# The prologue of a time-mix and mixture-of-experts kernel: low weight parts by subtraction, and the residual added by TensorE

## The reference

```python
for i in range(2):                                   # time mix, layer i
    normed = layer_norm(out, ln_w[i], ln_b[i])
    k, v = normed @ Wk[i].T, normed @ Wv[i].T
    r = sigmoid(normed @ Wr[i].T)
    state_t = 0.95 * state_{t-1} + 0.05 * (k * v)_t   # a scan over the tokens
    out = out + (r * state) @ Wo[i].T
x = layernorm(h + out)
# experts: each token goes to its 2 best experts of 8, each expert takes the first 307 rows
logits = x @ router_w + router_b
h_e = einp @ w_c_fc[e] + b_c_fc[e];  g_e = einp @ w_gate[e] + b_gate[e]
o_e = silu(h_e * g_e) @ w_c_proj[e] + b_c_proj[e]
x = layernorm(x + sum over the token's 2 experts of prob * o_e[its row])
```

## Time and profile before

| | |
|---|---|
| time before, median of 3 runs | 372.24 us (372.0 to 374.78) |
| the profiled execution's own time | 371.38 us |
| its span, first to last instruction | 369.4 us |
| PE busy | 331.3 us, 90% |
| DVE busy | 262.7 us, 71% |
| POOL busy | 194.9 us, 53% |
| ACT busy | 169.9 us, 46% |
| mean granted clock of TensorE | 0.983 of full speed |

### The profile page before, as it was taken

The page is one execution under the profiler, slowest core; times in us unless marked ns, Lnnn a source line. Parts: engine busy times, 40 slices in busy tenths (PEclk is TensorE's granted clock), DMA queues, the critical chain, the costliest instruction groups (busy, mean ns, idle before and its releaser), DMA issues.

```text
span 369.4 us, 7109 instructions
## 1 busy us (share of the span) xinstructions
PE 331.3 (90%) x2295; PEld 281.0 (76%) x2295; DVE 262.7 (71%) x851; ACT 169.9 (46%) x311; POOL 194.9 (53%) x240
## 2 busy tenths in 40 slices
PE   6979768678799999999999999999998999998980
PEld 2435354336697988999879879999998989988880
DVE  5487865757986677797868876989454688675535
ACT  1634425445454455455543635455554455555200
POOL 4021216871405565233346567784777755777762
PEclk9999979999999999999999999999999999999997
DMA  7902892435001311431111237222326712121152
GB/s 200 228 24 88 73 286 85 138 102 141 9 18 35 91 38 52 112 93 35 39 51 34 84 124 178 74 59 68 94 75 168 127 40 56 40 51 41 45 162 70
DMA packets 61245, 32.59 MB, mean 88 GB/s; under 512 B 15995, under 2 KB 58823, under 8 KB 61210
## 3 DMA queue, kind: packets, MB, share of 16 engines
q1 hardware_dynamic: 55866, 23.96, 26.9%
q0 software_dynamic: 4256, 7.94, 7.6%
q10 hardware_dynamic: 1088, 0.26, 0.4%
HBM read 19.01 MB, written 13.69 MB: 89 GB/s over the span
## 4 chain that ended last, share of the span: by engine, by line
PE 74%; DVE 9%; issue 5%; ACT 4%; POOL 3%; DMA 3%; POOLq 0%; DVEq 0%; ACTq 0%
PE ps_o L790 19%; PE bank L635 3%; PE pair1h L719 3%; PE bank L643 3%; PE bank L645 3%; PE pair1g L773 2%; PE pair0g L773 2%; PE ps_o L660 2%; DVE kv_sb L1096 2%; PE bank L751 2%; PE pair0g L774 2%; PE pair0g L775 2%; PE pair1g L775 2%; PE pair1g L774 2%; PE bank L615 2%
## 5 line engine op out<-in xcount | busy, mean ns | idle before, releaser
L790 PE MATMUL ps_o<-proj_sb,hidden 128*104 128x128 f32 x768 | 96.2, 273 | 0.2 <-DVE o_sb L1277 0.2
L1463 POOL DMA_INDIRECT slot_rows<-x_rows,row_to x64 | 71.4, 1116 | 42.5 <-DVE prod L1265 24.0
L790 PEld LDWEIGHTS ps_o<-proj_sb,hidden 128*104 128x104 f32 x768 | 90.2, 170 | 1.1 <-issue 0.7
L959 ACT ACTIVATE gate_s<-pair0g,bgate_sb 128x308 f32<-128x308 f32 x64 | 33.1, 517 | 73.6 <-PE pair0g L775 73.6
L1503 POOL DMA_INDIRECT picked<-expert_rows,row_from x48 | 49.8, 1037 | 31.0 <-DVE prod L1265 19.2
L1265 DVE SCALAR_TENSOR_TENSOR prod<-pair1h,bfc_sb,gate_s 128x308 f32<-128x308 f32 x64 | 34.0, 531 | 22.9 <-ACT gate_s L959 22.8
L966 ACT ACTIVATE hidden<-prod 128x616 f32<-128x616 f32 x64 | 45.5, 711 | 8.4 <-DVE prod L1265 8.4
L1265 DVE SCALAR_TENSOR_TENSOR prod<-pair0h,bfc_sb,gate_s 128x308 f32<-128x308 f32 x64 | 34.1, 532 | 14.7 <-ACT gate_s L959 14.2
L959 ACT ACTIVATE gate_s<-pair1g,bgate_sb 128x308 f32<-128x308 f32 x64 | 32.9, 515 | 24.0 <-PE pair1g L775 23.4
L1435 POOL TENSOR_SCALAR shifted<-moments 128x4 f32<-128x4 f32 x24 | 5.5, 231 | 69.0 <-DVE moments L1053 68.9
L773 PE MATMUL pair1g<-slotT_hi,gate_hi 128*128 128x308 f32 x64 | 26.0, 406 | 2.3 <-DVE prod L1265 2.2
(11 more groups left out here) (203 smaller groups left out, 766.3 us busy)
## 6 DMA issues: line engine op xcount, KB each, us to landing
slot_in<-slot_rows SPq DMA_DIRECT2D x20, 260.0 KB, 3.8
expert_rows<-o_sb SPq DMA_DIRECT2D x24, 156.0 KB
x_in<-in_L_attn_h SPq DMA_DIRECT2D x4, 512.0 KB, 5.2
x_rows<-in_L_ffn_w_gate SPq DMA_DIRECT2D x8, 256.0 KB, 4.2
...
```

Of the source, the lines that this page charges most:

```text
L790: mm = nc.tensor.matmul(ps_o[0:PART, P * part:P * part + P], hidden[:, e % 2, c, PART * part:PART * part + PART], proj_sb[:, e, c, :], sta ...
L959: nc.scalar.activation(gate_s[:, c % 2, :], pair[c % 2][0][:, 0:COLS], ACT.Identity, bias=bgate_sb[:, e, j:j + 1]).then_inc(g_copied, 1)
L1463: nc.gpsimd.indirect_dma_start(out=slot_rows, out_offset=bass.IndirectOffsetOnAxis(ap=row_to[:, c:c + 1], axis=0), in_=x_rows[:, b, c // K ...
```

## The change

It alters the prologue alone, and the tables of the periods stay. Its parts:

1. **Low parts by subtraction.** `split` on TensorE, `low` on ScalarE and the constant `minus` are gone. GpSimd subtracts for experts 0 and 1 and VectorE for experts 2 to 7, two subtractions of 128 by 512 for each expert (weight minus high part, all in SBUF). `high` is one entry for each matrix now. Loads of later experts wait for these subtractions.
2. **The residual added in PSUM.** A new stage `carry` on TensorE multiplies the residual by `ident` into the bank in which `out` then accumulates. Layer 1 needs 4 such products of 128 columns, layer 2 needs 8, since it adds `x_in` and `x_mid` (so `skip_sum` is gone for batches 0 and 1). `stats` reads the bank directly, and a new stage `added` on ScalarE copies it to SBUF in place of VectorE's `add`. Batch 0 alternates between two banks, `pair1h` and `ps_o`, and batch 1 uses the banks of its v products.
3. **Both halves turned first.** `turn` for both halves stands ahead of the two `kvr`, VectorE's `add` no longer stands between the halves, and the two turns and logits of the router have two banks.
4. **Order and fillers.** `FILL` has 18 fillers behind the first 12, in place of 23. `stats` of batch 2 moves from points 1 and 3 of the first period to the head of VectorE, and `stats` (1, 5) ahead of the slots. `load_x(2)` stands ahead of the loads of experts 4 to 7, and `load_expert(3)` behind the small biases.

The diff, cut to its core (of the lists a line each):

```diff
-TENSOR_HEAD = [("turn", 0, 0), ("kvr", 0, 0), ("turn", 0, 1), ("kvr", 0, 1), ("out", 0, 0), ("split", 0, 0),
+TENSOR_HEAD = [("carry", 0, 0), ("turn", 0, 0), ("carry", 0, 1), ("turn", 0, 1), ("kvr", 0, 0), ("kvr", 0, 1),
...
+               ("out", 0, 0), ("out", 0, 1), ("carry", 0, 2), ("turn", 0, 2), ("turn", 0, 3), ("kvr", 0, 2),
...
+               ("low", 7, 1), ("stats", 2, 0), ("stats", 2, 1), ("slots", 0, 0), ("slots", 0, 1),
...
+LOW_BY_POOL = 2
...
-FILL = {("weights", 0, 0): 12, ("turn", 0, 0): 5, ("kvr", 0, 0): 5, ("kvr", 0, 1): 1, ("turn", 0, 2): 3,
-        ("kvr", 0, 2): 4, ("kvr", 0, 3): 1, ("turn", 0, 4): 2, ("turn", 0, 5): 2}
+FILL = {("weights", 0, 0): 12, ("turn", 0, 0): 1, ("turn", 0, 3): 3, ("turn", 0, 4): 6, ("turn", 0, 5): 2, ("count", 0, 0): 6}
...
             if b >= 2:
                 return bank[1 + n % 2]
-            return ps_o
+            if b == 0:
+                return (pair[1][1], ps_o)[n % 2]
+            return mix_banks(b, n)[2]
...
-            return (ps_o,) * 3 if b == 0 else bank
+            return (pair[1][1], ps_o, pair[1][1]) if b == 0 else bank
...
             def load_expert(e):
-                if e >= 2:
-                    sp.wait_ge(weights_apart, 2 * (e - 1))
+                if 2 <= e < LOW_BY_POOL + 2:
+                    sp.wait_ge(pool_low_made, 2 * (e - 1))
+                elif e >= 2:
+                    sp.wait_ge(vector_low_made, 2 * (e - 1 - LOW_BY_POOL))
...
+            def carry(b, n):
+
+                if b == 1:
+                    pe.wait_ge(kv_made, step(b, n))
+                if n == 0:
+                    pe.wait_ge(x_loaded[b], 16)
+                if n > 1:
+                    pe.wait_ge(x_added, step(b, n - 2))
+                ps = out_bank(b, n)
+                for j in range(HT):
+                    t = HT * (n % 2) + j
+                    nc.tensor.matmul(ps[:, P * j:P * j + P], ident[:, :], x_in[:, b, t, :],
+                                     start=(j == 0), stop=False, skip_group_check=True)
+                    if n > 1:
+                        nc.tensor.matmul(ps[:, P * j:P * j + P], ident[:, :], x_mid[:, b, t, :],
+                                         start=False, stop=False, skip_group_check=True)
...
-                                          w_mix[:, 3 * L + n // 2, :], start=True, stop=True)
+                                          w_mix[:, 3 * L + n // 2, :], start=(b > 1), stop=True,
+                                          skip_group_check=(b < 2))
...
-            def split(e, which):
...
+            def added(b, n):
+
+                last = (n + 2) // 4
+                act.wait_ge(stats_made[last], step(b, n + 2))
+                act.wait_ge(out_made, step(b, n))
+                dst = x_mid if n < 2 else x_in
+                nc.scalar.activation(dst[:, b, HT * (n % 2):HT * (n % 2) + HT, :],
+                                     out_bank(b, n)[:, :].rearrange("p (j d) -> p j d", d=P), ACT.Copy)\
+                  .then_inc(x_added, 1)
...
-            def high(e, _):
+            def high(e, which):
...
-            def low(e, which):
...
-                    i = nc.vector.bn_stats(stats[:, r, norm, j, :], source_of(b, n)[:, j, :])
+                    i = nc.vector.bn_stats(stats[:, r, norm, j, :],
+                                           out_bank(b, n - 2)[:, P * (j % HT):P * (j % HT) + P] if summed
+                                           else source_of(b, n)[:, j, :])
...
+            def low_of(e, which):
+
+                dve.wait_ge(weights_high, 2 * e + which + 1)
+                nc.vector.tensor_tensor((gate_lo, fc_lo)[which][:, e, :].rearrange("p (j d) -> p j d", d=P),
+                                        w_in[:, e % 2, HC * which:HC * which + HC, :],
+                                        (gate_hi, fc_hi)[which][:, e, :].rearrange("p (j d) -> p j d", d=P).bitcast(F32),
+                                        ALU.subtract).then_inc(vector_low_made, 1)
...
-                    if b == 0 and point in (1, 3):
-                        stats_of(2, point // 2)
...
+            def low_of(e, which):
+
+                pool.wait_ge(weights_high, 2 * e + which + 1)
+                if e == 0:
+                    pool.wait_ge(state_made, step(0, 1))
+                else:
+                    pool.wait_ge(normed_made[0], step(0, 3))
...
```

152 lines of the change are left out of this document (74 added, 78 removed).

## The result

| | before | after |
|---|---|---|
| time, median | 372.46 us (372.0 to 374.78, 4 runs) | 363.89 us (363.4 to 364.26, 4 runs) |
| ratio | | 0.9771, 95% interval 0.9744 to 0.9797 |
| the profiled execution's own time | 371.38 us | 364.26 us |
| its span | 369.4 us | 362.4 us |
| first expert product starts | 90.48 us | 82.50 us |

The forecast was 363.5.

A forecast was written before the change was run, and what follows sets the result against it. TensorE, 90% busy, bounds the kernel, so gains lie in the prologue's waits. First product -8.7, holes -2.6, clock +2.3, VectorE's queue +0.3 sum to -8.7: profiled run 362.7, median 0.9 above, thus 363.5; range 360 to 368.

The forecast's parts named there:

- Batch 0's mixing: Prologue, batch 0's two layers: layer 1's norm ends 3.2 us earlier, layer 2's last norm 6.8 earlier, at 39.0.
- Routing: Prologue, router behind batch 0's mixing: logits end at 41.6, 8.5 us earlier; row numbers at 48.1, 8.4 earlier.
- Scatters: GpSimd's 16 scatters: 25.0 us as before plus 0.6 for VectorE's subtractions; slots loaded at 76.0, landed 79.2.
- GpSimd is dear: Rival: GpSimd's subtraction costs 2.4 or VectorE's subtractions stretch scatters by 4.4: 366 to 367.5, both 369 to 370; chance 0.18.
- Batch 1: Prologue: its last `out` ends at 72.4, or up to 5 us later by the clock (77.4), hidden by the slots at 79.2.
- The first product: Start of the expert stage: the first expert product starts at 81.8 against 90.48, -8.7 us.
- The holes: First period: TensorE's waits of 1.41 and 1.17 us behind VectorE close, -2.6.
- The clock in the last gap: TensorE idle from 73 to 79: clock falls to 1.2 GHz until about 86, slowing the first products, +2.3 us.
- After that the shift stays to the end: Periods behind the first points: TensorE is full as before, so the -8.7 us stays to the end.
- the periods take it back: Rival: the expert stage waits for something that doesn't move, up to 6 of the 8.7 us lost: 369.5; chance 0.05.
- The slower rival: Batch 1 in the prologue: the clock stays at 1.2 GHz throughout, 14 us left unhidden: about 375; chance 0.05.

The follow-up runs named there:

- the run at 371.4: The changed kernel with the two `rstd` of batch 1's second layer back behind the 10th and the 12th scatter: 371.41 us, ratio 0.9987.
- the run at 390: The kernel before with only the low parts by subtraction (no `split`, no `low` on ScalarE), all else as before: 390.08 us, ratio 1.0486.

## Why the prediction was right, point by point

- **Batch 0's mixing: right.** kv started at 14.30 (14.4 forecast), `mixed` of the second half ended at 19.77 (19.8), the norm of layer 2 at 25.74 (25.4), `out` at 35.17 (35.0), the last norm at 39.11 (39.0). GpSimd's subtraction took 1.18 (1.2), the first 1.69. By GPSIMD Engine Reference of the Trainium skill (Engine selection) twice VectorE's 0.61 would be 1.2, and the trace agrees to within the choice of VectorE's figure: its own subtraction of this size takes 0.68, and 1.18 is 1.7 times that. The 0.1 for statistics read from PSUM was 0.02 (0.89 for 0.87).
- **Routing: 0.7 late.** The logits were read at 41.74 (41.6), `row_to` was done at 48.82 (48.1). Six fillers put ahead of `count` were issued just as the clock fell and took 2.74 us, 0.9 beyond the moment that `chosen` was ready. The prediction costed fillers at nothing.
- **Scatters: the rhythm right, the contention mis-sized.** They took 25.9 us for 25.6 forecast, but the sum was luckier than its terms. VectorE's subtractions cost 1.6 (0.38, 0.30, 0.71 and 0.19 on the rows at 58.60, 59.29, 63.54 and 73.24) where I took 0.6. The 25.0 carried over from before is the plain 20.0, 2.6 for the two `rstd`, and 2.3 of stretched scatters that the prediction didn't name; in the changed kernel these last came to some 1.6, which hid most of the miss. Other runs of nearly the same kernel read 25.1 to 27.0, with scatters that begin under a scan among the long ones. The rival "GpSimd is dear" thus had a right mechanism at 1.6, less than half of the 4.4 that it put on it.
- **Batch 1: right.** Its last `out` ended at 76.17, inside 72.4 to 77.4, and with fillers ahead of its second layer 73.6. That it hides behind the scatters was shown by those fillers, and that it depends on the place of `rstd` by the run at 371.4.
- **The first product: 0.7 late** (82.50 for 81.8), by the row numbers and scatters.
- **The holes: right.** From the first product to the fifth point it took 7.55 us before, 5.51 in the changed kernel and 5.17 with the clock at 1.00 (16 fillers ahead of the slots): 2.4 without the clock's price, for 2.6 forecast. With the clock's term the prediction had this stretch 0.3 shorter; it is 2.0 shorter.
- **The clock in the last gap: right in place, wrong in size.** It read 0.50 from about 80.4 to 83.8; the price of 2.3 was 0.5 in this kernel (9.3 us from the first transpose to the 5th `prod` with the fall, 8.8 without), and 1.0 to 1.4 in the four profiles in which it lasted until about 86 and the statistics stood ahead. ScalarE's `gate_s` ends VectorE's last waits ahead of the 5th `prod` (0.27 and 0.74), so other engines limit the first points as well, which I had not counted.
- **"After that the shift stays to the end": wrong.** 3 us of 10.1 were given back, 1.2 and 1.4 of them in two stretches in which a code load meets a transfer. The rival "the periods take it back" named another cause, a wait for something that doesn't move. This step and the last one cancel: -8.7 forecast, -10.1 at the 5th `prod`, -7.0 in the span. The closeness of 363.5 to 363.9 is in part luck for a second reason: the profiled execution was forecast at 362.7 and took 364.26, and the 0.9 that was added for the median belonged to the profile of before; in the changed kernel the median lies 0.4 below the profiled execution.
- **The slower rival** (the clock low through all of batch 1) didn't come: 0.50 lasted 6 us. What can turn the change into a loss is another thing, the chain of weight buffers through three engines in the run at 390, which I had not seen.
